# Sorting a graph kernel's row tiles from the fewest neighbours to the most

## The reference, cut to what matters

```python
def reference(x, adj, W, a0, a1):
    h = relu(layernorm(x))                       # layer 0
    Wh = h @ W
    e = (Wh @ a0[:256])[:, None] + (Wh @ a0[256:])[None, :]
    x = x + leaky(softmax(where(adj == 0, -1e9, e)) @ Wh, 0.2)
    h = relu(layernorm(x))                       # layer 1
    e = leaky((h @ a1[:256]) + (h @ a1[256:]).T, 0.01)
    return x + softmax(where(adj > 0, e, -9e15)) @ h
```

## Time and profile before

| | us |
|---|---|
| median of 3 runs | 1716.38 |
| the profiled execution | 1716.22 |
| its span, first to last instruction | 1714.0 |
| first stage | 0 to 1068 |
| second stage, group 0 of the dense chunks on PE | 1083 to 1228 |
| second stage, groups 1 to 5 on PE | 1233 to 1704 |

### The profile page before, as it was taken

The page is one execution under the profiler, slowest core; times in us unless marked ns, Lnnn a source line. Parts: engine busy times, 40 slices in busy tenths (PEclk is TensorE's granted clock), DMA queues, the critical chain, the costliest instruction groups (busy, mean ns, idle before and its releaser), DMA issues. The chain is left out here.

```text
span 1714.0 us, 37172 instructions
## 1 busy us (share of the span) xinstructions
PE 1559.3 (91%) x13443; PEld 1327.4 (77%) x13443; DVE 1258.1 (73%) x4759; ACT 992.5 (58%) x1514; POOL 557.3 (33%) x588
## 2 busy tenths in 40 slices
PE   6877999999999999999999997585599999899877
PEld 5646888888888888888888886464488888787666
DVE  7577998998899889987864443596676766666556
ACT  5878656665666566657666641675454444444342
POOL 0000000000000000000035561576677777777774
PEclk9998999999999999999999999897799999999989
DMA  9418989988988898889899973745444444444433
GB/s 315 165 44 346 352 299 340 345 309 306 363 329 298 311 367 318 299 316 377 325 343 398 388 277 79 165 133 143 111 133 123 129 117 133 116 139 117 127 110 91
DMA packets 141698, 406.89 MB, mean 237 GB/s; under 512 B 25857, under 2 KB 91586, under 8 KB 108834
## 3 DMA queue, kind: packets, MB, share of 16 engines
q1 hardware_dynamic: 116114, 335.11, 53.5%
q0 software_dynamic: 25488, 70.77, 14.8%
HBM read 365.39 MB, written 40.41 MB: 237 GB/s over the span
## 5 line engine op out<-in xcount | busy, mean ns | idle before, releaser
L1006 PE MATMUL banks<-HV,adjT 128*128 128x257 f16 x8192 | 940.0, 274 | 16.6 <-DVE adjT L665 9.1
L1006 PEld LDWEIGHTS banks<-HV,adjT 128*128 128x128 fp8e4 x8192 | 793.3, 98 | 148.5 <-DVE HV L695 22.9
L1746 PE MATMUL banks<-Vp,adjp 128*128 128x257 f16 x2304 | 454.2, 279 | 97.2 <-DVE adjp L1560 79.8
L450 ACT ACTIVATE adj_f<-adj_i 128x2048 fp8e4<-128x2048 int32 x256 | 480.2, 1897 | 5.4 <-DMA adj_i<-in_adj 5.1
L1331 POOL DMA_INDIRECT gat<-h_of_layer,rec x393 | 415.0, 1056 | 149.3 <-issue 111.4
L1746 PE MATMUL banks<-Vn,adjn 128*128 128x257 f16 x2304 | 453.6, 279 | 0.0
L1746 PEld LDWEIGHTS banks<-Vp,adjp 128*128 128x128 fp8e4 x2304 | 226.0, 99 | 142.7 <-DVE Vn L1520 64.9
L432 POOL DMA_DIRECT2D xr<-x_after_layer x46 | 26.3, 572 | 832.4 <-DVE rank L933 772.3
L1746 PEld LDWEIGHTS banks<-Vn,adjn 128*128 128x128 fp8e4 x2304 | 228.8, 99 | 37.9
L1367 ACT ACTIVATE adjn<-h1bc,nh 128x384 fp8e5<-128x384 f32 x384 | 205.0, 605 | 35.5 <-PE banks L1746 31.1
L1619 DVE SCALAR_TENSOR_TENSOR sacc<-gat,w,sacc 128x257 f32<-128x257 f32 x347 | 156.7, 478 | 0.0
(11 more groups left out here) (172 smaller groups left out, 1484.3 us busy)
## 6 DMA issues: line engine op xcount, KB each, us to landing
adj_i<-in_adj SPq DMA_DIRECT2D x256, 1024.0 KB, 7.0
h_of_layer<-hh SPq DMA_DIRECT2D x64, 129.0 KB, 6.3
hs<-h_of_layer SPq DMA_DIRECT2D x64, 129.0 KB, 2.7
xt<-in_x SPq DMA_DIRECT2D x64, 128.0 KB, 6.7
packed_adj<-pk SPq DMA_DIRECT2D x64, 128.0 KB, 6.1
x_after_layer<-x SPq DMA_DIRECT2D x64, 128.0 KB, 6.6
HV<-in_x SPq DMA_DIRECT2D x14, 512.0 KB, 8.8
gat<-h_of_layer,rec POOLq DMA_INDIRECT x393, 2.8
```

Of the source, the lines that this page charges most:

```text
L450: nc.scalar.activation(adj_f[:, b, q * QC:(q + 1) * QC], adj_i[:, q, :], ACT.Copy, scale=2.0, saturate=False).then_inc(conv_done, 1)
L1006: last = nc.tensor.matmul(acc[b][:, 0:DV], adjT_h[:, b, i, q, :, h], V0[:, jb, s, 0:DV], start=(jb == 0 and s == 0), stop=(jb == T - 1 and ...
L1746: mm = nc.tensor.matmul(bank[2 * i + part][:, 0:DV], m[:, i * P:(i + 1) * P], V[:, j, s, 0:DV], start=(j == 0 and s == 0), stop=(j == T - ...
```

## The change

The list of slot counts is reversed, so that tile 0 has 3 slots and tile 45 has 23, and rank r becomes 5887 - r, so that the nodes with the fewest neighbours come first. `caps` is made from the same function and is reversed too. Nothing else is changed: batches, `rows_by` and the four queues are made by the same code from the reversed list.

```diff
@@ slot_counts
         counts.append(c)
-    return counts
+    return counts[::-1]
@@ sort_ranks
-    nc.vector.tensor_scalar(rank[:, :], rsum[:, :], -1.0, None, ALU.add)\
+    nc.vector.tensor_scalar(rank[:, :], rsum[:, :], -1.0, float(NS * P), ALU.mult, ALU.add)\
         .then_inc(rank_ready, 1)
```

## The result

The changed kernel takes **1739.38 us** (median of 4 runs, 1739.24 to 1740.45) against 1716.60 for the kernel before on the same chip (1716.27 to 1717.51): a ratio of **1.0133 [1.0116, 1.0151]**, 1.3% slower. The profiled execution took 1739.5 us, its span 1737.3.

A forecast was written before the change was run, and what follows sets the result against it. POOL was taken to bound groups 1 to 5, record loads waiting for stores group 0: first later gather 1258.7 + 417 + 44 + 2 = 1722, plus 18.6 = 1741 span, so 1743 us, 1.6% slower; range 1722 to 1772.

The forecast's parts named there:

- the nine chunks that were named: Group 0, chunks 6 to 12, 14 and 15: h tiles stand behind record loads waiting for stores, nine stalls for three.
- The releases: SP's queue in group 0: times when waiting record loads get their buffer, from 1137.6 (chunk 6) to 1246.4 us (chunk 15).
- The start: Chunk 6: row of chunk 3 done at 1119.0, ten gathers 14.9, two stores 1.3 + 2.4, released at 1137.6 us.
- the loop at chunk 12: Group 0: second row behind chunk 11 at 1210.3, released 1221.6 us; a loop of 20 us serves one chunk.
- The price of a gather: POOL in group 0: 1.49 us each with the issue gap, the old mean; bounds 1.25 and 4.0 us.
- the rule of the Trainium skill: Shared DVE/GpSimd port: twelve gathers ahead of chunks 11 and 12 would cost 1.25 us each, the sum ending 3 us lower.
- Where PE stands still: PE in group 0: idle ahead of chunks 6 to 12, 14 and 15, longest at 11 and 12.
- Groups 1 to 5: POOL is the bound: 316 gathers at 1.32 (417 us), 33 stores (44), 2 of waits; last gather ends at 1722.
- The tail: From the last gather to the span's end: 18.6 us along PE instead of 23, two stores behind instead of five.
- No waits: Rival: record loads in SP's queue don't wait for stores, POOL alone limits group 0, 1705 us; 8 in 100.
- The full loops: Rival: in steps 5 to 8 four more chunks take 20 us instead of 11, 1777 us; 11 in 100.
- A gain that cancels the loss: Rival: no change, group 0 growing by only 4 us and later savings as counted; 6 in 100.

The follow-up runs named there:

- after_eight: The changed kernel with eight result buffers instead of four, record loads asked for as early as before: 1697.74 us, ratio 0.9897.
- after_h8: The changed kernel with eight h tile buffers instead of four, h loads issued one chunk earlier, ahead of the record load: 1709.01 us, ratio 0.9973.
- before_eight: The kernel before the change with eight result buffers instead of four, record loads asked for as early as before: 1697.17 us, ratio 0.9907.

## Why the prediction was right

**What bounds the kernel, and the mechanism: right.** The h tiles of the nine chunks that were named stood behind a waiting record load, with ten waits of SP and 105 us (80 to 120 was forecast); POOL waited 67.8 us for rows (some 60 was forecast) and hardly rested from batch 16 on, at 1.31 us a transfer. after_eight and after_h8 show the cause, by taking away the wait and what stood behind it. Two counts beside the sum were off without effect on it: the 76 rows of group 0 reach into tile 4 before and into tile 14 now, not 5 and 13.

**The releases** (the start of SP's record load, or of the second of the two ahead of chunk 6): all nine within 6.9 us, and all early.

| chunk | 6 | 7 | 8 | 9 | 10 | 11 | 12 | 14 | 15 |
|---|---|---|---|---|---|---|---|---|---|
| predicted | 1137.6 | 1147.8 | 1159.4 | 1169.6 | 1181.2 | 1201.2 | 1221.6 | 1238.0 | 1246.4 |
| measured | 1131.3 | 1140.9 | 1154.6 | 1163.3 | 1178.8 | 1196.9 | 1215.3 | 1236.0 | 1243.4 |

Three terms were too big. The start: the step took the row that frees batch 5 from chunk 3 as it ran before, at 1119.0; now the gathers behind it began at 1114.05, and that is 5.0 of the 6.3 us at chunk 6. Then the loop at chunk 12: from release to release 18.4 us instead of 20.4. From the release to the first gather it took 7.9 (1196.91 to 1204.78) instead of 9.1, as the h tile landed in 2.13 us instead of the 3.70 of the earlier trace rows. And the six gathers took 8.1 (1204.78 to the end of the sixth, 1212.60, and a gap of 0.30) instead of 8.9.

**The price of a gather** is the third: 1.40 us over group 0 (77 gathers, 84.4 us, and 0.30 each), not 1.49 (before, 83 gathers, it was 1.50). The step took the old mean on the ground that both kinds would occur in the proportion in which DVE works; in the new group 0 DVE stands still for longer (it waits 44.1 us for ACT's high halves, 31.8 before), and the cheap kind is commoner: 6 of 77 gathers took over 1.5 us, 12 of 83 before. By the rule of the Trainium skill ("SBUF — State Buffer", Who interferes with whom) the gathers ahead of chunks 11 and 12 were to cost 1.25 each, and 10 of the 12 did. The first of each six, which runs beside the last additions of the chunk, took 1.57 or 1.58 with its gap on top. The mean of the 12 is 1.36, so between the two prices the rule was the nearer by little.

**Where PE stands still: partly wrong.** PE's idle time was to be longest ahead of 11 and 12. It was 12.29 us ahead of 6, and 9.94 and 11.04 there. The releases say why the step failed: a loop that serves two chunks puts nearly its whole wait ahead of the first of them (12.29 and 1.09 at 6 and 7, 8.82 and 0.46 at 8 and 9, 4.87 and 0.68 at 14 and 15), and I had spread it over both. As the sum went by releases, this cost nothing.

**Groups 1 to 5**: 463 us were forecast, 460.5 measured, by a pace of 1.31 for 1.32 and hardly any waits. What I named as given back there, eight more stores done in group 0, has a counterweight that I counted in the sum but didn't name: six gathers moved the other way, 8 us for 11.

**The tail**: 19.0 for 18.6, in part by luck. The sum took it along PE, and the chain does end there, but PE's last two chunks ended 11.0 us after the last gather (1729.4) instead of 9.2, and from there to the end it was 7.9 instead of 9.5: two misses of opposite sign. Before, those 9.5 us also held DVE's last sums for the stores, as the chain of before shows. What I said of the stores did not hold. Before, six of them followed the last gather and not five, and before_eight has six as well and needs 15.9, so their number is not the reason. Nor did POOL's waits between them go: one of 8.27 us is left, for 10.0 in four pieces before, but it runs beside PE.

**The rivals.** No waits: that kernel was worked out at 1705, and after_eight, where the waits are taken away, ran 1697.74, with POOL's first gather at 1218.7 for 1220. It was nearly the right price for a thing that didn't happen. The full loops (1777, by its own terms 1779: four times 9 us) stayed out, as the plan of rows said: chunks 7 and 9 followed 9.6 and 8.7 us behind 6 and 8. A gain that cancels the loss did not come: 2.5 and 4.2 us of 30.

## What to carry to other kernels

A queue that works in order turns one transfer's wait for a buffer into a wait of everything behind it: ahead of any reordering, list which waits move ahead of which loads, and follow one turn of that loop with durations from the trace. Three cures worked here, each by itself: ask for the waiting load one step later, put the loads of the next step ahead of it, or give it buffers so that it hardly waits (ratios to the kernel before of 0.9964, 0.9973 and 0.9897, from 1.0133). Only then does the order of the work show its own price: with eight result buffers none that can be measured, with six and a fifth batch buffer 5.6 us the other way.

## What the runs showed of the hardware

**The long gathers all began beside a closed run of DVE's two-input instructions, but half of the gathers beside such a run were short.** The 3.67 us gather of the earlier trace rows began at 1145.16 and ended at 1148.83. DVE's timeline of the kernel before meanwhile:

```profile
1145.15 0.48 DVE L1520 SCALAR_TENSOR_TENSOR Vp<-hs,Es,Vp 128x258 f16<-128x258 f32 x1
1145.55 0.47 DVE L1520 SCALAR_TENSOR_TENSOR Vn<-hs,Es,Vn 128x258 f16<-128x258 f32 x1
...
1146.74 1.27 DVE L1619 SCALAR_TENSOR_TENSOR sacc<-gat,w,sacc 128x257 f32<-128x257 f32 x3
...
1148.01 0.47 DVE L1619 SCALAR_TENSOR_TENSOR sacc<-gat,w,sacc 128x257 f32<-128x257 f32 x1
```

Each of these reads two tiles and lasts 0.48 us at most, and they stand back to back up to 1148.48; only a w of 0.15 us lies between; the mask instruction of L1555 comes next. The rule of the Trainium skill cited above speaks of one instruction that the other engine waits for; this gather stayed out through most of a run of them. Yet the same run of DVE began at 1141.82, and the two gathers ahead of this one, inside it, were short:

```profile
1142.60 1.00 POOL L1331 DMA_INDIRECT gat<-h_of_layer,rec  x1 [0.30 <-issue]
1143.90 0.96 POOL L1331 DMA_INDIRECT gat<-h_of_layer,rec  x1 [0.30 <-issue]
```

A count over the gathers of group 0, before and after the change together: 52 began with no two-input instruction (SCALAR_TENSOR_TENSOR or TENSOR_TENSOR) on DVE in their first 0.95 us, and none of them took over 0.98 us. 66 began with DVE full of them for that time; 33 of these took 1.00 us or less, and 18 took 1.57 to 3.67, which are all of those over 1.5 us. The 42 in between took 1.32 at most. So in these traces such a run goes with every long gather, but doesn't make one by itself. It is a coincidence of rows and was not tried by itself; what decides between the two is open.

**An h tile landed faster while POOL stood still.** In the chains of waits between 1130 and 1250 us, four h tiles after the change landed 2.13 to 2.37 us after their issue with POOL at rest, and five, before and after, took 3.44 to 4.42 while it issued gathers (3.70 in the earlier trace rows). Two earlier ones don't fit: 2.27 beside gathers (after, 1083.93), and 7.70 of which POOL gathered only for the first 1.7 us (before, 1100.60). So this isn't a measurement of that contention; but the term was the largest miss of the loop.
